# Softplus by ScalarE's table, the scan started three wide tiles earlier, and the context normalization moved into the first two tiles

## The chip, the cores and the metric

The kernel runs on one core of a Trainium2 chip. Its time is the device time of that core in microseconds (us); the median of three runs before the change is 1597.76 us (1597.14 to 1597.82). The core has five engines that run side by side and wait for one another through semaphores: TensorE (PE; its weight loads are PEld), VectorE (DVE), ScalarE (ACT), GpSimd (POOL) and SyncE (SP). Each takes its own instructions strictly in the order of the program. DMAs are started from the queues of SP, ACT and POOL.

## The reference, cut to what matters

One decoder layer on four sequences of 512 tokens, width 512: attention, then a selective state-space branch, then a gated feed-forward with routed low-rank adapters. The part that the change touches is the state-space branch:

```
x    = silu(conv(in_proj(ctx)))                    # 512 channels x 512 tokens
dt   = softplus(dt_proj(x_proj(x)[:16]) + dt_bias)
A    = -exp(A_log)                                 # 16 states for each channel
for each token:
    state = state * exp(dt * A) + (dt * u) * B
    y     = sum over the 16 states of state * C
y    = (y + D * x) * silu(layernorm(tokens after attention))
```

The first stage of each sequence is `layernorm(x)`, the input of attention.

## The kernel before, in words

A batch is one of the four sequences. All data are f32. Each batch b passes these stages:

1. Input projection, convolution, B, C and the step sizes dt (`conv_tap`, `convolve`, `conv_gate`, `split_first`, `softplus_parts`).
2. Projections of q, k and v with rotation (`project`, `rotate`), in 11 places f.
3. Attention: 32 steps, two heads in each (`attention`). In a step PE computes scores, DVE takes the maxima (L1117), ACT takes exponentials (L622), PE transposes (L830), ACT moves (L634), and PE weighs the values.
4. Feed-forward, of 11 wide tiles f = 0..10 of 128 columns ("wide tile"). For each tile PE forms `base` (L890, 16 matmul instructions), then two adapter slots (L902, 4 instructions each), and `down_adapters` (L910, 4). ACT takes a silu (L674) and DVE a product (L1253) after each of these three; such a pair is an evaluation, named (f, 0), (f, 1), (f, 2). Its place in the order is (0,0), (0,1), (1,0), (0,2), (1,1), (2,0), (1,2) and so on; `EVAL` holds it. PE's `base(f+2)` waits for the product of (f, 2), since both use the same PSUM banks.
5. Down products (L970), 11 places f, and a last one (L977), after which DVE adds the residual (L1266, `finish`).

Batch b+1's stages 1 and 2 and its scan run beside batch b's stages 4 and 5: stage 1 at the head of the feed-forward, the scan's pieces in DVE's and ACT's gaps from there on, stage 2's projections between the down products (one f of each), and the rest of the scan in batch b+1's attention. Batch 0 has nothing to hide behind: its scan runs beside its own projections and attention.

The scan of a batch goes over its 16 states n. For each n DVE does three pieces over 128 x 2048: mul (L1077, dt*u times B), run (L1082, the recurrence), out (L1087, times C). Then a DMA from POOL's queue adds the result to y (L484); the adds of a batch are serial, and the state has two buffers, so mul n waits until add n-2 has landed. ACT makes the decay factors of each n with four exponentials (L580), and loads B and C of each n by DMA (L570). Both wait in ACT's order for pieces of n-2. Ahead of the 48 scan pieces stand 12 "poly" pieces on DVE: softplus as max(v, 0) + log(1 + exp(-|v|)), where ACT gives |v|, its exponential and max(v, 0) (L546, L549, L551), and DVE evaluates a polynomial of degree 9 in Horner's form (L1051, nine times L1054), adds the two parts (L1059), and forms dt*u (L1063).

The order is fixed by tables written out by hand: `plan(counts)` deals the 60 pieces of a batch in order into slots, so many to each, and puts the loads and decays of n in a slot between the pieces that free and use their buffers, after an evaluation (f, 1) if one lies between. `PLAN_NEXT` (batches 1 to 3) has no piece before the fifth evaluation slot, from then on 2 pieces after (f, 1) and 1 after (f, 2), 22 pieces beside the down products, and the last 8 in attention. `PLAN_FIRST` (batch 0) has 13 pieces beside the projections, 10 of them in the first two places, and 47 in attention's first 31 steps. The normalization of batch b+1's attention input (`deviation`, L1014 to L1020, POOL's power L474, `scaled`, L1024) stands in `NORM_SLOTS`: one of four token tiles after (5, 2), (6, 2), (7, 2) and (8, 2) each.

## Time and profile before

| | |
|---|---|
| median of 3 runs | 1597.76 us |
| the profiled execution, its own time | 1596.27 us |
| its span in the profile | 1594.5 us |
| busy: PE, DVE, ACT, POOL | 1382.6, 1108.9, 689.2, 112.0 us |
| mean granted TensorE clock | 0.888 of full |

In order of time, batch 0's projections and attention fill about 0 to 270 us; then three periods of some 370 us follow, each with a feed-forward head (from 272 us), wide tiles (310 to 450), down products (450 to 527), attention of the next batch (536 to 620) and gating; the last feed-forward alone runs from 1390 to the end. A row of the timeline gives start, duration, engine, line, operation, output <- inputs, and how many instructions were merged; in brackets stands the idle time of the engine before it and what ended it. PE's clock stands at one of two levels, 2.4 GHz (1.00 in the rows) or 1.2 GHz (0.50).

### The profile page before, as it was taken

What the parts mean: (1) busy time and instruction counts of PE and PEld (TensorE: products, weight loads), DVE (VectorE), ACT (ScalarE), POOL (GpSimd) and SP (SyncE); (2) the same over time, 40 slices, a digit from 0 to 9 for tenths busy, and PEclk for the clock granted to TensorE, in tenths of its full rate; (3) what the DMA queues carried; (4) which work ended last, traced back from release to release, by engine and by line L of the source; (5) the groups of instructions that cost most, each with busy time, mean ns of one, the idle gap of its engine ahead of it and who ended that gap; (6) DMA issues with size and microseconds to landing.
All of it is one profiled execution on the core that took longest, in us unless ns stands there. A gap on an engine that the chain in (4) does not pass through costs nothing.

```text
span 1594.5 us, 16051 instructions
## 1 busy us (share of the span) xinstructions
PE 1382.6 (87%) x5768; PEld 675.0 (42%) x5768; DVE 1108.9 (70%) x1247; ACT 689.2 (43%) x1501; POOL 112.0 (7%) x116
## 2 busy tenths in 40 slices
PE   6756667999988799899989699899989698799999
PEld 2334334444443355434444255444434255454443
DVE  4899996557989775737999866637998967621120
ACT  6155653344543484343552376361562277321110
POOL 0000001000200000000210000100210000100000
PEclk8955558999999699999999778999999869789999
DMA  4166662114667631113766722002566751101112
GB/s 191 40 152 157 141 142 50 42 50 112 172 145 172 171 68 27 40 35 81 180 147 159 196 67 54 27 32 80 141 150 152 169 139 28 27 19 61 50 35 84
DMA packets 53277, 158.80 MB, mean 100 GB/s; under 512 B 5072, under 2 KB 10704, under 8 KB 44752
## 3 DMA queue, kind: packets, MB, share of 16 engines
q0 software_dynamic: 9216, 67.11, 20.4%
q1 hardware_dynamic: 25664, 54.23, 10.1%
q10 hardware_dynamic: 18320, 36.45, 8.6%
q8 instruction: 47, 0.77, 0.2%
q14 instruction: 30, 0.25, 0.0%
HBM read 86.20 MB, written 4.46 MB: 57 GB/s over the span
## 4 chain that ended last, share of the span: by engine, by line
issue 30%; PE 29%; DVE 26%; DMA 7%; ACT 5%; POOL 2%; ACTq 0%; DVEq 0%; POOLq 0%
DVE state L1082 10%; DMA y_sb<-state 7%; PE ps_a L890 5%; PE ps_a L970 4%; DVE state L1077 4%; PE ps_w L869 3%; DVE state L1087 3%; PE ps_a L816 3%; PE ps_a L902 2%; PE ps_b L830 2%; ACT r L622 2%; POOL rstd L474 2%; DVE neg_max L1117 2%; PE ps_b L910 2%; PE ps_w L778 2%
## 5 line engine op out<-in xcount | busy, mean ns | idle before, releaser
L890 PE MATMUL ps_a<-xt,w_sb 128*128 128x512 f32 x704 | 316.1, 603 | 0.0
L1082 DVE TENSOR_TENSOR_SCAN state<-decay,state 128x2048 f32<-128x2048 f32 x64 | 282.8, 4419 | 7.5 <-ACT decay L580 3.4
L1253 DVE TENSOR_TENSOR r<-r,ps_a 128x512 f32<-128x512 f32 x132 | 88.6, 683 | 206.4 <-ACT r L674 206.4
L816 PE MATMUL ps_a<-r 32*128 32x512 f32 (+3 forms) x512 | 140.6, 634 | 84.0 <-ACT r L622 57.5
L890 PEld LDWEIGHTS ps_a<-xt,w_sb 128*128 128x128 f32 x704 | 135.6, 194 | 171.1 <-issue 171.1
L674 ACT ACTIVATE r<-ps_a 128x512 f32<-128x512 f32 x132 | 78.4, 597 | 297.8 <-PE ps_a L902 158.7
L580 ACT ACTIVATE decay<-dt_sb,decay_rate 128x511 f32<-128x511 f32 x256 | 163.0, 712 | 63.2 <-DVE state L1087 31.2
L622 ACT ACTIVATE r<-ps_a,neg_max 128x128 f32<-128x128 f32 (+3 forms) x256 | 133.8, 534 | 118.7 <-DVE neg_max L1117 118.3
L902 PE MATMUL ps_a<-r,wb_sb 128*128 128x512 f32 x352 | 166.7, 596 | 11.1 <-DVE r L1253 8.9
L970 PE MATMUL ps_a<-wd_sb,r 128*128 128x512 f32 x352 | 161.8, 611 | 0.8 <-DMA wd_sb<-in_w_down 0.8
L1077 DVE TENSOR_TENSOR state<-du_sb,bc_sb 128x2048 f32<-128x2048 f32 x64 | 146.3, 2287 | 5.2 <-DMA y_sb<-state 5.0
L1087 DVE TENSOR_TENSOR state<-state,bc_sb 128x2048 f32<-128x2048 f32 x64 | 146.0, 2281 | 0.7
L830 PE MATMUL ps_b<-cst,r 128*128 128x128 f32 x640 | 120.4, 331 | 25.6 <-ACT xt L634 17.2
L1117 DVE TENSOR_REDUCE neg_max<-ps_a 128x2 f32<-128x256 f32 (+3 forms) x128 | 104.0, 814 | 19.9 <-PE ps_a L819 19.0
L484 POOL DMA_DIRECT2D y_sb<-state x64 | 56.1, 877 | 738.1 <-DVE state L1087 653.4
L902 PEld LDWEIGHTS ps_a<-r,wb_sb 128*128 128x128 f32 x352 | 64.9, 190 | 101.9 <-issue 95.1
L970 PEld LDWEIGHTS ps_a<-wd_sb,r 128*128 128x128 f32 x352 | 69.1, 198 | 88.7 <-issue 84.0
L830 PEld LDWEIGHTS ps_b<-cst,r 128*128 128x128 f32 x640 | 89.1, 172 | 34.5 <-issue 28.7
L816 PEld LDWEIGHTS ps_a<-r 32*128 32x128 f32 x512 | 50.2, 239 | 120.7 <-ACT r L622 79.7
L474 POOL TENSOR_TENSOR rstd<-var_eps,cst 128x1 f32<-128x1 f32 x48 | 56.0, 1167 | 543.7 <-DVE var_eps L1020 534.3
L910 PE MATMUL ps_b<-r,ad_sb 128*128 128x512 f32 x176 | 85.8, 611 | 1.9 <-DVE r L1253 1.7
L1054 DVE SCALAR_TENSOR_TENSOR du_sb<-du_sb,state 128x2048 f32<-128x2048 f32 x36 | 82.4, 2288 | 0.6
(123 smaller groups left out, 1448.4 us busy)
## 6 DMA issues: line engine op xcount, KB each, us to landing
y_sb<-state POOLq DMA_DIRECT2D x64, 1024.0 KB, 9.7
bc_sb<-bc_rows ACTq DMA_DIRECT2D x64, 512.0 KB, 5.1
w_sb<-in_w_tiles SPq DMA_DIRECT2D x44, 512.0 KB, 4.0
wd_sb<-in_w_down SPq DMA_DIRECT2D x44, 256.0 KB, 3.6
wb_sb<-in_w_adapt SPq DMA_DIRECT2D x44, 128.0 KB, 2.1
xa<-in_x SPq DMA_DIRECT2D x4, 1024.0 KB, 5.2
out_x<-xb SPq DMA_DIRECT2D x16, 256.0 KB, 7.0
xn_att<-in_ctx_t SPq DMA_DIRECT2D x4, 512.0 KB, 6.1
```

The lines of the kernel that those rows point to most:

```text
L580: nc.scalar.activation(decay[:, n % 2, j, 1:L], dt_sb[:, j, 1:L], ACT.Exp, scale=decay_rate[:, j, n:n + 1]).then_inc(decay_ready, 1)
L622: nc.scalar.activation(probs[:, (2 * s + k) % 4, 0:(i + 1) * P], score_place(s, k), ACT.Exp, bias=neg_max[:, s % 2, k:k + 1], accum_out=ro ...
L816: nc.tensor.matmul(score_place(s, k), q_t[rows, m, i * P:(i + 1) * P], k_t[rows, 0:width], start=True, stop=False, tile_position=(rows.sta ...
L830: mm = nc.tensor.transpose(ps_b[:, k, kt * P:(kt + 1) * P], probs[:, (2 * s + k) % 4, kt * P:(kt + 1) * P], ident)
L890: mm = nc.tensor.matmul(ps_a[:, 2 * (f % 2) + half, :], w_sb[:, slot, at + k * P:at + (k + 1) * P], xt[:, k, :], start=(k == 0), stop=Fals ...
L902: mm = nc.tensor.matmul(ps_a[:, 2 * (f % 2) + half, :], wb_sb[:, f % 2, at:at + P], low[:, 2 * half + k - 1, :], start=False, stop=(k == 2 ...
L910: mm = nc.tensor.matmul(ps_b[:, k - 1, :], ad_sb[:, f, :], hk[:, (2 * f + k - 1) % 4, :], start=(f == 0), stop=(f == FT - 1), skip_group_c ...
L970: mm = nc.tensor.matmul(ps_a[:, i, :], hb[:, f, i * P:(i + 1) * P], wd_sb[:, f % 2, :], start=(f == 0), stop=False, skip_group_check=True)
L1077: tt(state[:, n % 2, :, :], du_sb[:], row, ALU.mult).then_inc(scan_chain, 1)
L1082: nc.vector.tensor_tensor_scan(flat, decay[:, n % 2, :, :].rearrange("p j l -> p (j l)"), flat, 0.0, ALU.mult, ALU.add).then_inc(scan_chai ...
L1087: tt(state[:, n % 2, :, :], state[:, n % 2, :, :], row, ALU.mult).then_inc(scan_chain, 1)
L1117: nc.vector.tensor_reduce(neg_max[:, s % 2, :], both, AX.X, ALU.max, negate=True)\
```

## The change

- Softplus is one ScalarE activation for each channel tile, straight from PSUM into `dt_sb`. The 12 poly pieces become one, "du", which forms dt*u; 49 pieces are left of 60. The scratch uses of `exp_v` and `relu_v` go.
- For batches 1 to 3 the first piece comes after (1, 1): two pieces there, none after (1, 2), and from tile 2 on 2 after (f, 1) and 1 after (f, 2) as before. 29 pieces stand there (30 before), 13 beside the down products (22 before), 7 in attention (8 before).
- For batch 0: one piece in each of the 11 places beside the projections, 38 in attention (47 before).
- The normalization of the next attention input is done in two pairs of token tiles, after (0, 1) and after (0, 2).

```diff
-    pieces = [("poly", k) for k in range(NPOLY + 2)]
+    pieces = [("du", 0)]
...
-        slots[between(at["poly", NPOLY - 4] if n < 2 else at["out", n - 2], at["mul", n])]["bc"].append(n)
-        slots[between(at["poly", NPOLY + 1] if n < 2 else at["run", n - 2], at["run", n])]["decay"].append(n)
+        slots[at["du", 0] if n < 2 else between(at["out", n - 2], at["mul", n])]["bc"].append(n)
+        slots[between(at["du", 0] if n < 2 else at["run", n - 2], at["run", n])]["decay"].append(n)
...
-NORM_SLOTS = [EVAL_AT[FT - 2 - NT + i, 2] for i in range(NT)]
+NORM_AT = {EVAL_AT[0, 1]: (0, 1), EVAL_AT[0, 2]: (2, 3)}
...
-IN_EVALS = [(0, 2, 1)[k] if e >= POLY_AT and f <= LAST_TILE else 0 for e, (f, k) in enumerate(EVAL)]
-IN_DOWN = 22 
+IN_EVALS = [0 if f == 0 else ((0, 2, 0) if f == 1 else (0, 2, 1))[k] for f, k in EVAL]
+IN_DOWN = 13
...
-            def softplus_parts(b, tiles):
+            def softplus(b, tiles):
                 for j in tiles:
                     bank = filled(act, ("dt", j), b)
...
+                    nc.scalar.activation(dt_sb[:, j, :], ps_w[:, bank, :], ACT.Softplus,
+                                         bias=vec[:, V_DTB + j:V_DTB + j + 1]).then_inc(work_free[bank], 1)
...
+                if kind == "du":
+
+                    for j in (JT - 2, JT - 1):
+                        bank, count = use(("dt", j), b)
+                        dve.wait_ge(work_free[bank], count + 1)
+                    dve.wait_ge(u_ready, b * JT + JT)
+                    tt(du_sb[:], dt_sb[:], u_sb, ALU.mult).then_inc(du_ready, 1)
+
+                    nc.vector.memset(decay[:, :, :, 0:1], 0.0).then_inc(dt_ready, 1)
...
-                    if e in NORM_SLOTS:
+                    for i in NORM_AT.get(e, ()):
                         dve.wait_ge(loaded["x"], 16 * t + 32)
-                        deviation("att", t + 1, xa, NORM_SLOTS.index(e))
+                        deviation("att", t + 1, xa, i)
+                    for i in NORM_AT.get(e, ()):
+                        scaled("att", t + 1, xa, xn_att, i)
                     for piece in PLAN_NEXT[e]["dve"]:
                         scan_piece(t + 1, piece)
-                    if e in NORM_SLOTS:
-                        scaled("att", t + 1, xa, xn_att, NORM_SLOTS.index(e))
```

How this moves the instructions, at three places. First, ACT between the evaluations of tiles 0 and 1 of a feed-forward; L674 is a silu before the change, L549 the exponential of softplus. Before:

```order
L674 ACTIVATE r<-ps_a 128x512 x2
L546 ACTIVATE state<-ps_w,vec 128x512
L549 ACT_TABLE_LOAD
L549 ACTIVATE state<-state 128x512
L551 ACTIVATE decay<-ps_w,vec 128x512
L546 ACTIVATE state<-ps_w,vec 128x512
L549 ACTIVATE state<-state 128x512
L551 ACTIVATE decay<-ps_w,vec 128x512
L674 ACT_TABLE_LOAD
L674 ACTIVATE r<-ps_a 128x512
```

After it; L642 is the silu, L522 the softplus, L548 a decay, L538 the loads of B and C:

```order
L642 ACTIVATE r<-ps_a 128x512
L522 ACT_TABLE_LOAD
L522 ACTIVATE dt_sb<-ps_w,vec 128x512 x2
L642 ACT_TABLE_LOAD
L642 ACTIVATE r<-ps_a 128x512
L538 DMA bc_sb<-bc_rows 128x2x512 x2
L642 ACTIVATE r<-ps_a 128x512
L548 ACT_TABLE_LOAD
L548 ACTIVATE decay<-dt_sb,decay_rate 128x511 x4
L642 ACT_TABLE_LOAD
L642 ACTIVATE r<-ps_a 128x512 x2
```

Three activations for each pair member became one, and the first decay stands after the silu of (2, 0), ahead of that of (1, 2); before the change the first decays stood behind the polynomial, four tiles later.

Second, DVE in the same tiles. Before (L1253 is the product of an evaluation, L1051 and L1054 are the polynomial):

```order
L1253 TENSOR_TENSOR r<-r,ps_a 128x512 x4
L1051 TENSOR_SCALAR du_sb<-state 128x2048
L1054 SCALAR_TENSOR_TENSOR du_sb<-du_sb,state 128x2048
L1253 TENSOR_TENSOR r<-r,ps_a 128x512 x2
L1054 SCALAR_TENSOR_TENSOR du_sb<-du_sb,state 128x2048
L1253 TENSOR_TENSOR r<-r,ps_a 128x512
L1054 SCALAR_TENSOR_TENSOR du_sb<-du_sb,state 128x2048 x2
```

After (L1211 is the product, L992 ends a normalization pair, L1021 is du, L1035, L1040 and L1045 are mul, run and out):

```order
L992 TENSOR_SCALAR xn_att<-xa,mv,rstd 128x512 x2
L1211 TENSOR_TENSOR r<-r,ps_a 128x512
L1021 TENSOR_TENSOR du_sb<-dt_sb,state 128x2048
L1023 MEMSET decay 128x8
L1035 TENSOR_TENSOR state<-du_sb,bc_sb 128x2048
L1211 TENSOR_TENSOR r<-r,ps_a 128x512 x3
L1040 SCALAR_TENSOR_TENSOR state<-decay,state 128x2048
L1045 TENSOR_TENSOR state<-state,bc_sb 128x2048
L1211 TENSOR_TENSOR r<-r,ps_a 128x512 x2
L1035 TENSOR_TENSOR state<-du_sb,bc_sb 128x2048
L1211 TENSOR_TENSOR r<-r,ps_a 128x512
```

The scan's first pieces stand where the polynomial's stood, and each tile from the third on has run and out after one product, mul after the next two.

Third, DVE at the end of the down products, from the last rotation (L1103 before, L1061 after) to the residual sum of `finish` (L1266, L1224). Before:

```order
L1103 TENSOR_TENSOR r<-r 128x512
L1082 SCALAR_TENSOR_TENSOR state<-decay,state 128x2048
L1087 TENSOR_TENSOR state<-state,bc_sb 128x2048
L1077 TENSOR_TENSOR state<-du_sb,bc_sb 128x2048
L1082 SCALAR_TENSOR_TENSOR state<-decay,state 128x2048
L1108 COPY v_sb<-ps_b 128x256
L1087 TENSOR_TENSOR state<-state,bc_sb 128x2048
L1077 TENSOR_TENSOR state<-du_sb,bc_sb 128x2048
L1082 SCALAR_TENSOR_TENSOR state<-decay,state 128x2048
L1087 TENSOR_TENSOR state<-state,bc_sb 128x2048
L1077 TENSOR_TENSOR state<-du_sb,bc_sb 128x2048
L1266 TENSOR_TENSOR xb<-ps_a,xb 128x512 x4
```

After:

```order
L1061 TENSOR_TENSOR r<-r 128x512
L1045 TENSOR_TENSOR state<-state,bc_sb 128x2048
L1035 TENSOR_TENSOR state<-du_sb,bc_sb 128x2048
L1040 SCALAR_TENSOR_TENSOR state<-decay,state 128x2048
L1066 COPY v_sb<-ps_b 128x256
L1045 TENSOR_TENSOR state<-state,bc_sb 128x2048
L1035 TENSOR_TENSOR state<-du_sb,bc_sb 128x2048
L1040 SCALAR_TENSOR_TENSOR state<-decay,state 128x2048
L1224 TENSOR_TENSOR xb<-ps_a,xb 128x512 x4
```

Ten pieces between the last rotation and `finish` became seven, and fewer stand ahead of that rotation. PE's order is the same in both kernels; on POOL the powers of a batch's normalization now all stand ahead of its adds. SP's order is unchanged.

## Rows read from the trace of the kernel before

**Rows 1.** Part 1 of the page: engine, busy us, share, instructions.
```profile
PE 1382.6 (87%) x5768; PEld 675.0 (42%) x5768; DVE 1108.9 (70%) x1247; ACT 689.2 (43%) x1501; POOL 112.0 (7%) x116
```

**Rows 2.** Stretches: from:to, us, busy of PE, PEld, DVE, ACT, POOL; clock, DMA, GB/s.
```profile
78.00:120.00 42.00, 24.72 (x132) 12.95 (x132) 41.79 (x29) 25.39 (x68) 2.77 (x3) 0.57 0.59 145
...
450.50:514.50 64.00, 56.21 (x131) 24.41 (x129) 57.61 (x35) 17.97 (x28) 5.22 (x6) 0.97 0.67 160
...
536.00:558.60 22.60, 21.56 (x114) 11.02 (x114) 13.94 (x20) 14.97 (x48) 0.00 (x0) 0.50 0.58 178
558.60:575.00 16.40, 15.85 (x206) 10.07 (x202) 11.03 (x22) 13.25 (x49) 0.86 (x1) 1.00 0.42 98
```

**Rows 3.** Groups by line: instructions, busy us and mean ns, idle before.
```profile
L1082 DVE TENSOR_TENSOR_SCAN state<-decay,state 128x2048 f32<-128x2048 f32 x64 | 282.8, 4419 | 7.5 <-ACT decay L580 3.4
...
L1087 DVE TENSOR_TENSOR state<-state,bc_sb 128x2048 f32<-128x2048 f32 x64 | 146.0, 2281 | 0.7
...
L1054 DVE SCALAR_TENSOR_TENSOR du_sb<-du_sb,state 128x2048 f32<-128x2048 f32 x36 | 82.4, 2288 | 0.6
...
L674 ACT ACT_TABLE_LOAD x28 | 35.9, 1283 | 0.5
...
L546 ACT ACTIVATE state<-ps_w,vec 128x512 f32<-128x512 f32 x16 | 10.9, 680 | 1.1 <-PE ps_w L752 1.1
```

**Rows 4.** Timeline of batch 0: DVE's first rows, and POOL's second and last add.
```profile
36.37 1.23 DVE L1051 TENSOR_SCALAR du_sb<-state 128x2048 f32<-128x2048 f32 x1 [9.96 <-ACT scrap_a L555]
...
80.10 0.42 DVE L1117 TENSOR_REDUCE neg_max<-ps_a 128x2 f32<-128x256 f32 x1
...
98.19 0.88 POOL L484 DMA_DIRECT2D y_sb<-state  x1 [9.42 <-DMA y_sb<-state]
...
247.53 0.88 POOL L484 DMA_DIRECT2D y_sb<-state  x1 [9.35 <-DVE state L1087]
```

**Rows 5.** PE's timeline: `base` of wide tiles 4, 5, 8 and 9.
```profile
352.89 7.03 PE L890 MATMUL ps_a<-xt,w_sb 128*128 128x512 f32 x16
...
364.91 7.03 PE L890 MATMUL ps_a<-xt,w_sb 128*128 128x512 f32 x16
...
401.38 7.03 PE L890 MATMUL ps_a<-xt,w_sb 128*128 128x512 f32 x16
...
414.18 7.03 PE L890 MATMUL ps_a<-xt,w_sb 128*128 128x512 f32 x16
```

**Rows 6.** DVE's timeline: mul of three tiles; then POOL's powers, ns min/median/max.
```profile
417.61 2.29 DVE L1077 TENSOR_TENSOR state<-du_sb,bc_sb 128x2048 f32<-128x2048 f32 x1
...
430.40 2.29 DVE L1077 TENSOR_TENSOR state<-du_sb,bc_sb 128x2048 f32<-128x2048 f32 x1
...
441.19 2.28 DVE L1077 TENSOR_TENSOR state<-du_sb,bc_sb 128x2048 f32<-128x2048 f32 x1
...
L474 POOL TENSOR_TENSOR rstd<-var_eps,cst x12: 550/780/2531, 388.4 to 650.5; 128x1 f32<-128x1 f32 x12
```

**Rows 7.** Timeline: PE at the dt products in tile 0; ACT's decay in tile 7.
```profile
323.58 1.13 PE L752 MATMUL ps_w<-xdt_sb,wdt_sb 128*128 128x512 f32 x2 [0.72 <-ACT decay L551]
...
326.36 1.88 PE L902 MATMUL ps_a<-r,wb_sb 128*128 128x512 f32 x4
...
392.25 2.56 ACT L580 ACTIVATE decay<-dt_sb,decay_rate 128x511 f32<-128x511 f32 x4
```

**Rows 8.** PE's timeline at the end of the down products.
```profile
514.55 1.12 PE L799 MATMUL ps_b<-cst,r 128*128 128x128 f32 x4 [7.03 <-ACT r L608]
...
523.36 3.60 PE L977 MATMUL ps_a<-bd_sb,r 128*128 128x512 f32 x8
536.06 0.80 PE L816 MATMUL ps_a<-r 32*128 32x128 f32 x4 [9.10 <-DVE xb L1266]
```

**Rows 9.** PE's timeline late in that attention, around a wait.
```profile
608.82 1.24 PE L816 MATMUL ps_a<-r 32*128 32x512 f32 x4 [2.71 <-ACT r L622]
...
611.60 2.08 PE L816 MATMUL ps_a<-r 32*128 32x512 f32 x4
```

More of the change, by code:

```diff
@@ L43 @@
 VD = KV_HEADS * HD
-def log1p_coefficients(degree):
-    import numpy as np
-    nodes = 0.5 + 0.5 * np.cos(np.pi * (np.arange(64) + 0.5) / 64)
-    fit = np.polynomial.Chebyshev.fit(nodes, np.log1p(nodes) / nodes, degree, domain=[0, 1])
-    return [float(c) for c in fit.convert(kind=np.polynomial.Polynomial).coef]
-POLY = log1p_coefficients(9)
-NPOLY = len(POLY)
 EVAL = [(0, 0)]
@@ L72 @@
 SLOTS = ATT + STEPS
-NORM_SLOTS = [EVAL_AT[FT - 2 - NT + i, 2] for i in range(NT)]
+NORM_AT = {EVAL_AT[0, 1]: (0, 1), EVAL_AT[0, 2]: (2, 3)}
 DT_SLOTS = (2, 3)
-POLY_AT = 4
-LAST_TILE = FT - 1
 PV_AT = 5
@@ L256, in decoder_layer @@
         xdt_sb = sb("xdt_sb", [P, L])
-        u_sb, exp_v, relu_v, conv_sb = state[:, 0, :, :], state[:, 1, :, :], decay[:, 0, :, :], decay[:, 1, :, :]
-        xin_sb = relu_v
+        u_sb, xin_sb, conv_sb = state[:, 0, :, :], decay[:, 0, :, :], decay[:, 1, :, :]
         scrap = sb("scrap", [1, 1])
@@ L323, in decoder_layer @@
         bc_stored = sem("bc_stored")
-        softplus_chain = sem("softplus_chain")
-        softplus_in = sem("softplus_in")
         y_init = sem("y_init")
-        poly_chain = sem("poly_chain")
+        du_ready = sem("du_ready")
         dt_ready = sem("dt_ready")
@@ L500, in _ @@
                 for e in range(EVALS):
-                    inverse_deviation("att", t + 1, [i for i in range(NT) if NORM_SLOTS[i] == e])
+                    inverse_deviation("att", t + 1, NORM_AT.get(e, ()))
                     add_states(t + 1, PLAN_NEXT[e])
@@ L691, in _ @@
             split_first(0)
-            softplus_parts(0, range(JT))
+            softplus(0, range(JT))
             for f in range(FT):
@@ L712, in _ @@
                     scan_inputs(t + 1, PLAN_NEXT[e])
-                    softplus_parts(t + 1, [j for _, j in dt_uses(e)])
+                    softplus(t + 1, [j for _, j in dt_uses(e)])
                 for f in range(FT):
@@ L1070, in scan_piece @@
                     if n == 0:
-                        dve.wait_ge(poly_chain, (b + 1) * (NPOLY + 2))
+                        dve.wait_ge(du_ready, b + 1)
                         dve.wait_ge(y_init, b * JT + JT)
```

35 lines of the change are left out of this document (2 added, 33 removed).

## The prediction

> **What bounds the kernel now.** I read the page's first part, then a table of stretches by stage, then PE's and DVE's timelines where a stretch looked full. DVE is busy for only 70% of the span [rows 1], but that is a mean over unlike stages. In batch 0's attention it is busy 41.79 of 42.00 us while PE stands at about half its clock and is busy for 24.72 [rows 2]: DVE sets the pace, and stays full until its last scan piece ends at about 247 us, where the last add starts [rows 4]. In the wide tiles PE sets the pace, one tile in 364.91 - 352.89 = 12.02 us, except where the normalization stands: 414.18 - 401.38 = 12.80 us [rows 5]. Beside the down products DVE is busy 57.61 of 64 us, and PE twice waits for what is queued behind DVE's pieces: 7.03 us at the turning of v, 9.10 us before the first scores [rows 2, 8]. The attention that follows starts at half clock: 22.6 us for its first eight steps with PE busy 21.56, against 16.4 us for the next eight at full clock [rows 2]. The last feed-forward runs alone and is not touched.
>
> **The change part by part.**
>
> *Work removed.* Ten polynomial pieces and one addition leave each batch. The nine L1054 alone are 9 x 2.288 = 20.6 us a batch, 82.4 us in all [rows 3]. What this is worth depends on the stage.
>
> *Softplus.* No row shows this function. One activation from PSUM with a bias column takes 0.68 us (L546), the sequence of three now in place about three times that [rows 3]; it could be no cheaper than nothing. I take 0.68 us, since the shape and operands are those of L546; the upper end would cost 16 x 1.3 us more on ACT, on the path only in the first dozen, near 5 us in all. Each change of function set shows as one load of 1.283 us [rows 3]; 91 stand in the new order against 66.
>
> *Batch 0.* Now DVE starts the polynomial at 36.37 us, having waited 9.96 us, and takes the first maxima at 80.10 [rows 4]. After the change eight activations of some 0.55 us, overlaps taken off, leave ACT's row, so softplus ends about 4 us earlier, near 32.3, du (2.3 us) near 34.6, and then the projections pace DVE: B and C of n = 0 land near 42 us (their issue follows the four moves of the transposed tokens), the first two decays sit on ACT between the first and second q move, and out 1 falls near 73. mul 3 is the last piece before the maxima, and waits until add 1 has landed, one add later: adds follow each other in (247.53 - 98.19)/14 = 10.7 us [rows 4], so near 84, and it ends near 86.2. The first maxima come 6.1 us later than now. From there 38 pieces remain instead of 47: three runs, outs and muls fewer. A run is 4.42 us, an out 2.28 and a mul 2.29 [rows 3, 6], less an overlap of about 0.1 us each: 3 x 8.8 = 26.3 us. Balance -20.2 us; I take 1 us off for waits that show when each step holds less DVE work: **-19 us**. Bounds: -12 (DVE waits for PE at half clock) and -24 (the start loses nothing).
>
> *Wide tiles of batches 1 to 3.* Three terms.
> Softplus at tile 0: PE waits for free banks at the dt products (323.58) and starts the slot of (1, 1) at 326.36 [rows 7]; without waits the four groups end at 324.42, so PE would gain 1.9 us.
> It gives this back at once. The first decay stands between the silus of (2, 0) and (1, 2). It costs two loads and 2.56 us [rows 3, 7] = 5.1 us, so the product of (1, 2) is ready about 2.2 us after `base(3)` wants it. Balance at tile 3: -0.25 us. Bounds -2 and +3.
> The normalization leaves tiles 5 to 8: its three full tiles cost 0.78 us each over 12.02 [rows 5], the first, by the same difference, 0.42, together 2.75 us. In tile 0 a pair stands between two products with a `base` of 6.9 us of PE between them, where DVE has nothing else; each half of it costs what the tiles show, 2.0 us [rows 6], so a pair takes 4 us and is hidden.
> Tiles 2 to 4 trade polynomial for scan. A DVE cycle with three scan pieces and three products, no normalization, takes 441.19 - 430.40 = 10.8 us, with it 430.40 - 417.61 = 12.8 [rows 6]. 10.8 is below PE's 12.02. Inside a tile the product of (f+1, 0) comes after run and out, 8.9 us after the slot of (f, 1) ends; PE wants it at 10.3 (`base` 6.87, slot 1.72, adapters 1.72). Cover 1.4 us; nothing is lost. Together **-3.0 us** a batch.
>
> A power on POOL takes 0.55 us at best and 2.53 us in the tiles where DVE's out runs beside it [rows 6]. By the Trainium skill ("SBUF — State Buffer", "Who interferes with whom") a VectorE instruction with two SBUF inputs holds off a GpSimd one that reads SBUF; this trace agrees, and by that rule the moved powers, beside statistics of one input, take the short time.
>
> *Down products.* From PE's own work, matmul pairs at 0.86 us: after the place of the last raw projection but one nothing holds PE, so L799 comes at 507.4 (now 514.55), L977 at 515.1 (now 523.36, 1 us of it low clock) and ends at 518.5, on the clock of batch 1 [rows 8]. DVE has 13 pieces, 39 us, in a stage where it had 22. I followed it place by place: after the rotation of place 6 (500.6) come out 11 (502.9), mul 12, run 12 (509.6), the copy of v (510.0), out 12 (512.3). mul 13 waits for add 11, 502.9 + 10.7 = 513.6, and ends at 515.9; run 13 ends at 520.3. ACT loads B and C of 13 behind out 11 at 502.9, before the move of v is due at 503.9: it just fits. So the residual sums start at 520.3 and the first scores, which need two, at 521.7 against 536.06 [rows 8]: **-14.4 us**. Bounds: -9 (ACT's queue still holds v back) and -16.5 (PE's end decides). One weight load of the down products is late by 0.8 us today and stays so; the one of place 10 has only 4.3 us from its release and may be 3 us late, which DVE's end covers.
>
> *Attention of batches 1 to 3.* One run leaves the first eight steps, seven pieces remain. At half clock PE is bound there (21.56 of 22.6 us), so the run is worth about **-1 us**. If the clock stays full the eight steps take what the next eight do, -6.1 us. For a fall: a wait of 2.71 us late in the same attention, followed by scores on 32 rows, was enough; the same matmuls that had taken 1.24 us took 2.08 from 611.60 on [rows 9]. My timeline leaves PE idle for up to 3.2 us at this place, followed by the same sparse matmuls. I take a fall.
>
> **Sum.** -19 + 3 x (-3.0 - 14.4 - 1.0) = -19 - 55.2 = -74.2 us. The profiled execution took 1596.27 us (span 1594.5, 1.8 us around it), which gives 1522.1; the median is 1.5 us above the profiled execution, so 1523.5.
>
> **The rivals.**
> *The clock stays full after the shortened gap.* For it: the gap shrinks from 9.1 us to 3 or less, and to nothing if a late weight load fills it with work. Against it: rows 9. Worth 3 x 5.1 = 15.3 us more: 1508.
> *Only part of the down gain comes.* The queue of adds or ACT's loads, which wait in order for out n-2, hold the move of v or mul 13 by some 5 us; batch 0 meets the adds' pace and gains 12. For it: the margins above are 1 to 2 us, and DMA engines are 67% busy there [rows 2]. Sum: -12 - 3 x 13 = -51: 1546.
> *ACT becomes the bound by its loads.* 25 more loads are 32 us of ACT; at 1.28 us each they lie in silu gaps. If each switch held ACT twice as long, the stall of `base(3)` would grow by 2.6 us and the two softplus pairs by as much: 3 x 5.2 = 15.6 us, 1539. The rows speak against it: a decay group such as the one at 392.25 follows its load with no idle time before it [rows 7].
> By the Trainium skill ("ScalarE: Activation LUTs", "What ACT_TABLE_LOAD costs") a switch costs about 2.66 us, a drain on top of the load; the load itself agrees with the row, the drain is not seen here.
> *Slower.* The scan triple now stands in nine tiles more or less densely from tile 2 on, so 27 tiles depend on mul n finding add n-2 landed. Out ends 8.2 us into its tile, mul comes 22.0 us after that tile's start: an add may take 13.8 us. Now it takes 10.7 from one to the next [rows 4]. Were it 17.5 us, 27 tiles would lose 3.7 us each, 100 us, and the time would be 1624; below 13.8 nothing is lost. Break-even stands near 16.5 us.
>
> **How the numbers follow.** Forecast 0.56, clock full 0.26, partial gain 0.11, ACT bound 0.03, slower 0.02, and 0.02 for a gain eaten by something unseen. The range runs from the clock rival with a little more in batch 0 (1501) to the partial gain (1545) and leaves out less than 0.2; the forecast's own range is 1514 to 1534. About 0.2% is what a measurement of this kernel tells from none: faster 0.96, same 0.01, slower 0.03.
>
> **What would show it.** Batch 0: first maxima near 86, last scan piece near 227. Tiles: `base` every 12.02 us from tile 3 on, one PE wait of about 2 us before `base(3)`. Down: no wait of PE at the turning of v, first scores 14 us earlier, clock 0.50 in the steps after. The prediction fails if PE shows waits in every tile (then DVE or ACT is late), or if the last scan piece of batch 0 does not move by about 20 us.

## The result and the profile after

The changed kernel takes 1528.68 us (median of four runs, 1524.95 to 1531.99) against 1597.79 us of the kernel before in the same session: a ratio of 0.956, with a 95% interval from 0.952 to 0.959. The forecast was 1523.5 us, 5 us less. The profiled execution took 1529.66 us, its span 1527.9 us: 66.6 us less than before, where the sum said 74.2.

Part 1 of the page after, and the row below it on which engine stands on the chain that ended last. They answer to [rows 1].

```profile
PE 1373.7 (90%) x5768; PEld 678.7 (44%) x5768; DVE 1018.1 (67%) x1203; ACT 704.4 (46%) x1490; POOL 89.7 (6%) x116
...
PE 68%; DVE 19%; ACT 6%; DMA 3%; issue 3%; ACTq 0%; POOL 0%; DVEq 0%
```

DVE lost 91 us of work and ACT gained 15; PE's share of the chain is 68%. To see where the time went, I took the starts of four groups in PE's timeline (first scores, L784; output projection, L837; `base(0)`, L858; first down product, L938) in both traces, and subtracted stage by stage. The three figures of a stage are batches 1 to 3, or feed-forwards 0 to 2:

| stage | before, us | after, us | difference | forecast |
|---|---|---|---|---|
| batch 0 up to `base(0)` | 288.0 | 266.4 | -21.6 | -19 |
| wide tiles | 162.5, 164.0, 163.7 | 160.8, 160.9, 160.8 | -7.6 | -9.0 |
| down products up to the first scores | 85.6, 84.6, 85.4 | 70.1, 70.3, 70.8 | -44.5 | -43.2 |
| attention up to the output projection | 80.6, 81.4, 81.4 | 86.3, 82.5, 79.6 | +5.1 | -3.0 |
| gating and head | 41.2, 41.0, 42.9 | 41.0, 41.0, 42.2 | -0.9 | 0 |
| last feed-forward alone | 192.2 | 195.1 | +2.9 | 0 |

Three of four terms came within 3 us of the forecast. The fourth has the wrong sign. Attention's 32 steps, in groups of eight (start of the first scores to start of the next group's; the last group ends at the output projection), the three figures again batches 1 to 3:

| steps | before, us | after, us | difference |
|---|---|---|---|
| 0 to 7 | 22.5, 22.5, 22.5 | 20.2, 16.2, 14.7 | -16.4 |
| 8 to 15 | 16.4, 17.1, 17.3 | 19.0, 19.2, 19.7 | +7.2 |
| 16 to 23 | 19.2, 19.7, 19.8 | 18.6, 18.8, 17.3 | -4.1 |
| 24 to 31 | 22.4, 22.1, 21.8 | 28.4, 28.3, 27.9 | +18.3 |

Stretches of after, for the first eight steps of attention, the next three groups of eight (batch 1), and the first and last group of batch 3; then the kernel before's last group of batch 1. The columns are those of [rows 2].

```profile
497.34:517.56 20.22, 18.82 (x112) 9.82 (x113) 10.61 (x19) 13.78 (x47) 0.86 (x1) 0.62 0.76 222
517.56:536.60 19.04, 16.49 (x205) 10.67 (x201) 14.39 (x22) 13.27 (x49) 0.00 (x0) 0.95 0.01 2
536.60:555.22 18.62, 18.62 (x201) 12.39 (x201) 10.76 (x21) 15.16 (x53) 0.88 (x1) 0.82 0.29 59
555.22:583.65 28.43, 26.61 (x204) 15.35 (x200) 16.44 (x25) 17.29 (x57) 0.87 (x1) 0.59 0.05 10
...
1210.90:1225.60 14.70, 12.02 (x112) 6.55 (x112) 10.35 (x19) 11.68 (x43) 0.87 (x1) 1.00 0.71 220
...
1262.61:1290.50 27.89, 23.30 (x205) 14.03 (x201) 16.45 (x25) 16.99 (x57) 0.86 (x1) 0.70 0.05 11
```

```profile
594.18:616.62 22.44, 19.18 (x201) 11.77 (x201) 16.65 (x24) 16.46 (x57) 0.87 (x1) 0.85 0.03 7
```

The last eight steps take 28 us in all three batches where they took 22, with the same DVE work (16.44 against 16.65 us) and, in batch 1, 7.4 us more of PE: PE is not given more work, it runs at half clock for most of the group (0.59 on average). What stands in front of it is in the merged timeline of after, PE, DVE and ACT at the turn to that group:

```profile
553.64 2.27 DVE L1035 TENSOR_TENSOR state<-du_sb,bc_sb 128x2048 f32<-128x2048 f32 x1
...
555.83 1.22 DVE L1075 TENSOR_REDUCE neg_max<-ps_a 128x2 f32<-128x1024 f32 x1
...
557.08 0.69 ACT L590 ACTIVATE r<-ps_a,neg_max 128x512 f32<-128x512 f32 x1 [1.19 <-DVE neg_max L1075]
...
558.58 0.49 PE L784 MATMUL ps_a<-r 32*128 32x128 f32 x4 [1.78 <-ACT r L590]
...
562.35 1.22 PE L784 MATMUL ps_a<-r 32*128 32x256 f32 x4
```

A mul stands ahead of the maxima of the widest scores (1024 columns), so its exponential and with it the next narrow scores are late; PE idles 1.78 us, and the scores on 256 columns, four of which take 0.70 us at 2.4 GHz, take 1.22: 1.2 GHz from about there. In batch 3 the clock is low for a shorter part (0.70), and the group takes as long, since PE waits once more, behind the run at step 26:

```profile
1278.06 1.65 PE L784 MATMUL ps_a<-r 32*128 32x384 f32 x4 [2.78 <-ACT r L590]
```

Taking one piece out of attention had moved the others: `spread_over(8, 31)` put the last seven at steps 7, 11, 15, 19, 23, 27, 30, all but the last behind the second maxima of a pair; `spread_over(7, 31)` puts them at 4, 8, 13, 17, 22, 26, 30.

### The profile page after: what moved, and what is told of

It is laid out like the page before. It is cut to its first block, busy times and chain, and to the rows that moved or that the text cites. A ratio compares the mean times of both kernels' runs of the same rounds, so it can differ in the third digit from the quotient of the medians.

```text
span 1527.9 us, 15994 instructions
## 1 busy us (share of the span) xinstructions
PE 1373.7 (90%) x5768; PEld 678.7 (44%) x5768; DVE 1018.1 (67%) x1203; ACT 704.4 (46%) x1490; POOL 89.7 (6%) x116
## 3 DMA queue, kind: packets, MB, share of 16 engines
q0 software_dynamic: 9216, 67.11, 22.1%
q1 hardware_dynamic: 25664, 54.23, 10.6%
## 4 chain that ended last, share of the span: by engine, by line
PE 68%; DVE 19%; ACT 6%; DMA 3%; issue 3%; ACTq 0%; POOL 0%; DVEq 0%
PE ps_a L858 20%; PE ps_a L870 9%; DVE state L1040 7%; PE ps_a L938 7%; PE ps_b L878 5%; PE ps_a L784 4%; PE ps_w L746 4%; PE ps_w L837 4%; PE ps_b L798 3%; DMA y_sb<-state 3%; DVE state L1035 2%; DVE neg_max L1075 2%; PE ps_w L904 2%; PE ps_w L813 2%; ACT r L590 2%
## 5 line engine op out<-in xcount | busy, mean ns | idle before, releaser
L858 PE MATMUL ps_a<-xt,w_sb 128*128 128x512 f32 x704 | 318.7, 607 | 6.4 <-DVE r L1211 6.4
L1040 DVE TENSOR_TENSOR_SCAN state<-decay,state 128x2048 f32<-128x2048 f32 x64 | 282.6, 4416 | 1.3
L858 PEld LDWEIGHTS ps_a<-xt,w_sb 128*128 128x128 f32 x704 | 136.5, 195 | 180.1 <-issue 180.1
L1211 DVE TENSOR_TENSOR r<-r,ps_a 128x512 f32<-128x512 f32 x132 | 90.2, 685 | 188.5 <-ACT r L642 188.5
L642 ACT ACTIVATE r<-ps_a 128x512 f32<-128x512 f32 x132 | 78.4, 596 | 268.2 <-PE ps_a L858 122.5
L548 ACT ACTIVATE decay<-dt_sb,decay_rate 128x511 f32<-128x511 f32 x256 | 163.3, 710 | 71.0 <-DVE state L1040 70.6
L784 PE MATMUL ps_a<-r 32*128 32x512 f32 (+3 forms) x512 | 138.7, 626 | 54.5 <-ACT r L590 50.6
L938 PE MATMUL ps_a<-wd_sb,r 128*128 128x512 f32 x352 | 156.6, 594 | 8.1 <-DMA wd_sb<-in_w_down 8.1
L1035 DVE TENSOR_TENSOR state<-du_sb,bc_sb 128x2048 f32<-128x2048 f32 x64 | 146.0, 2282 | 10.2 <-DMA bc_sb<-bc_rows 5.2
L1045 DVE TENSOR_TENSOR state<-state,bc_sb 128x2048 f32<-128x2048 f32 x64 | 146.2, 2285 | 1.4
L798 PE MATMUL ps_b<-cst,r 128*128 128x128 f32 x640 | 123.7, 339 | 15.6 <-ACT r L602 9.2
L938 PEld LDWEIGHTS ps_a<-wd_sb,r 128*128 128x128 f32 x352 | 67.0, 192 | 93.3 <-issue 80.1
L798 PEld LDWEIGHTS ps_b<-cst,r 128*128 128x128 f32 x640 | 92.8, 178 | 22.1 <-issue 20.0
L784 PEld LDWEIGHTS ps_a<-r 32*128 32x128 f32 x512 | 49.2, 234 | 89.8 <-ACT r L590 66.0
L602 ACT ACTIVATE xt<-ps_b 128x256 f32<-128x256 f32 (+1 forms) x128 | 58.3, 500 | 26.3 <-PE ps_b L798 25.6
L1088 DVE TENSOR_TENSOR r<-ps_w,r 128x128 f32<-128x128 f32 x64 | 18.3, 286 | 68.1 <-ACT r L609 68.1
```

The source lines that it names most:

```text
L548: nc.scalar.activation(decay[:, n % 2, j, 1:L], dt_sb[:, j, 1:L], ACT.Exp, scale=decay_rate[:, j, n:n + 1]).then_inc(decay_ready, 1)
L784: nc.tensor.matmul(score_place(s, k), q_t[rows, m, i * P:(i + 1) * P], k_t[rows, 0:width], start=True, stop=False, tile_position=(rows.sta ...
L798: mm = nc.tensor.transpose(ps_b[:, k, kt * P:(kt + 1) * P], probs[:, (2 * s + k) % 4, kt * P:(kt + 1) * P], ident)
L858: mm = nc.tensor.matmul(ps_a[:, 2 * (f % 2) + half, :], w_sb[:, slot, at + k * P:at + (k + 1) * P], xt[:, k, :], start=(k == 0), stop=Fals ...
L938: mm = nc.tensor.matmul(ps_a[:, i, :], hb[:, f, i * P:(i + 1) * P], wd_sb[:, f % 2, :], start=(f == 0), stop=False, skip_group_check=True)
L1035: tt(state[:, n % 2, :, :], du_sb[:], row, ALU.mult).then_inc(scan_chain, 1)
```

## Experiments

All kernels are variants of the changed kernel. Medians are of 4 to 10 runs, ratios are to the kernel before on the same chip. The intervals reach 0.2 to 0.4% to either side: runs of one variant differ by 4 to 16 us, those of the kernel before on one chip by 23, and the longer ones mostly have the lower granted clock (after: 1524.95 us at 0.907, 1531.99 at 0.899). The median of the kernel before is 1596.6 to 1599.9 us on the four chips, so medians of two variants from different chips can lie 3 us apart for that alone.

**The attention pieces at the steps of before.**

```diff
-                 spread_over(PIECES - sum(IN_EVALS) - IN_DOWN, STEPS - LAST_STEPS) + [0] * LAST_STEPS)
+                 [int(s in (7, 11, 15, 19, 23, 27, 30)) for s in range(STEPS)])
```

> The changed kernel, with the same seven scan pieces of batches 1 to 3 in attention, now behind the maxima of steps 7, 11, 15, 19, 23, 27 and 30, where the kernel before had the same seven; the changed kernel has them at 4, 8, 13, 17, 22, 26, 30. Nothing else differs. Theory P (positions): in the changed kernel a mul behind the first wide step (22) and a run at 13 hold up the maxima of the next wide step, PE waits 1.8 and 2.6 us for exponentials at the narrow scores that follow, the granted clock falls there, and the last eight steps take 28 us. Then here the waits before the first scores of the third and fourth group of eight go below 0.6 us, the second group takes 16.5 us (now 19.0 to 19.7) and the last 22.4 (now 28), and the three attentions together take 20 to 25 us less: about 1506 us. Rival C (the clock falls for what came before attention): the waits go, but the low stretches stay, and the time is 1525 or more. Rival N: seven pieces cost what they cost, no attention gets shorter by over 1 us.

Measured 1511.91 us, ratio 0.947 (0.944 to 0.949): 17 us less than the changed kernel. Its four groups of eight in batch 1, and the first group of batch 3:

```profile
502.35:522.35 20.00, 18.81 (x113) 9.81 (x112) 9.52 (x18) 12.94 (x45) 0.00 (x0) 0.62 0.39 134
522.35:539.45 17.10, 16.60 (x204) 10.70 (x200) 11.06 (x21) 13.17 (x49) 0.86 (x1) 0.95 0.43 94
539.45:559.15 19.70, 17.82 (x202) 11.08 (x200) 14.48 (x22) 14.84 (x53) 0.88 (x1) 0.91 0.27 55
559.15:581.20 22.05, 18.81 (x208) 11.42 (x200) 16.67 (x24) 16.49 (x57) 0.87 (x1) 0.87 0.03 6
1202.38:1215.70 13.32, 11.92 (x114) 6.60 (x114) 8.43 (x18) 11.77 (x43) 0.00 (x0) 1.00 0.51 180
```

The last group is back at 22.05 us, the second at 17.1; the third gives back 1 us. Theory P (the positions) holds, in the size a little less than expected (17 us of 20 to 25; the three attentions are 18 us shorter together). The 8 us by which the attention term was off are this, and more.

**The normalization back in tiles 5 to 8.**

```diff
-NORM_AT = {EVAL_AT[0, 1]: (0, 1), EVAL_AT[0, 2]: (2, 3)}
+NORM_AT = {EVAL_AT[FT - 2 - NT + i, 2]: (i,) for i in range(NT)}
```

(and `scaled` again behind the scan pieces of the slot.)

> The changed kernel with the normalization of the next attention input back behind the evaluations (5,2), (6,2), (7,2) and (8,2), a token tile in each. The prediction's term: the period of base in those tiles goes from 12.02 to 12.8 us in three of them and 12.4 in one, 2.75 us a batch, about 8 us in all: 1537. Rival: since VectorE now also waits less elsewhere, or since the tiles' end is set by what follows them, nothing comes of it (1529), or, with the scan already running in these tiles as before, more than 4 us a batch (1541 or more).

Measured 1541.99 us, ratio 0.965 (0.961 to 0.969): 13 us more. Two stretches from one `base` to the next:

```profile
370.53:382.68 12.15, 12.15 (x30) 5.24 (x28) 11.59 (x12) 6.91 (x9) 2.86 (x3) 1.00 0.71 199
382.68:395.41 12.73, 12.26 (x30) 5.24 (x29) 12.17 (x12) 6.91 (x9) 3.43 (x3) 1.00 0.73 181
```

POOL's powers in these tiles (ns: least, median, most):

```profile
L451 POOL TENSOR_TENSOR rstd<-var_eps,cst x3: 2547/2547/2549, 382.5 to 407.9; 128x1 f32<-128x1 f32 x3
```

PE's timeline at the last down product of feed-forward 2:

```profile
1213.52 6.75 PE L938 MATMUL ps_a<-wd_sb,r 128*128 128x512 f32 x8 [2.73 <-DMA wd_sb<-in_w_down]
```

The period is 12.73 us as it was 12.80 [rows 5], and the wide tiles lose 2.0 us a batch, 5.9 in all: the term was 2.75 a batch. The three periods from `base(7)` to `base(10)` lose 1.6 of these 2.0. The profiled execution is 17.6 us longer than that of the changed kernel (it is the slowest of its four), and most of that is not in the tiles. The down products took 4.3 us more, where the clock fell, as the last row shows (eight matmuls in 6.75 us behind a late weight load; 3.7 us behind the same wait in the changed kernel). Attention took 4.3 us more: its first eight steps 20.2 us in all three batches, where the changed kernel's trace has 20.2, 16.2 and 14.7, and its last eight 26.4 instead of 28. Batch 0, which the edit does not touch, took 2.8 us more. So the time is that of the rival that expected over 4 us a batch, but the trace gives the place 2.0; whether the edit has a part in the rest is open. The powers stand beside a mul here, beside an out in the kernel before; in the changed kernel the powers beside the statistics took 0.547 to 0.782 us. By the Trainium skill ("SBUF — State Buffer", "Who interferes with whom") a VectorE instruction with two SBUF inputs contends with a GpSimd one that reads SBUF; both traces agree.

**The scan started late, 22 pieces beside the down products.**

```diff
-IN_EVALS = [0 if f == 0 else ((0, 2, 0) if f == 1 else (0, 2, 1))[k] for f, k in EVAL]
-IN_DOWN = 13
+IN_EVALS = [0 if f < 4 else ((0, 2, 0) if f == 4 else (0, 2, 1))[k] for f, k in EVAL]
+IN_DOWN = 22
```

> The changed kernel with the scan starting behind (4,1) instead of (1,1): 20 pieces in the wide tiles instead of 29, 22 beside the down products instead of 13, the same seven in attention at the same steps. Theory: the down products' 15 us a batch hang on the number of pieces there, since v's move and the residual sums stand behind them; the stage from the first down product to the first scores goes from 70.3 back to about 85 us, PE waits 7 us at the turning of v and 8 to 9 us before the first scores: 3 x 14.7 = 44 us more, 1573. Base(3) starts 2.1 us earlier, since no decay stands before it: 1567. Rival: part of the 15 us came from the queue of adds and from ScalarE's order, not from the count; then the stage stays under 78 us, 1550 or less.

Measured 1590.87 us, ratio 0.996 (0.994 to 0.998): 62 us more, so that nearly all of the change's gain is gone. The stage of the down products and the eight steps of attention behind it:

```profile
428.17:514.60 86.43, 67.61 (x160) 29.51 (x158) 80.29 (x44) 24.11 (x40) 6.08 (x7) 0.93 0.74 167
514.60:536.10 21.50, 21.24 (x114) 10.97 (x114) 10.53 (x19) 14.12 (x47) 0.86 (x1) 0.50 0.72 212
```

The stage takes 86.4 us as before the change: the number of pieces there decides, worth 16.3 us a batch, 49 in all. Against the expected 1567 the kernel is 24 us slower. The wide tiles, from which 6 us were to come, are 2.4 us longer together: the wait before `base(3)` is gone, but it moved with the scan's start to `base(6)`, which comes 14.31 us after `base(5)`, and the period after it takes 13.79 us. The attentions are 11 us longer together. Their first eight steps start at half clock and take 21.5 us; most variants with 13 pieces have 20.0 to 21.3, so the changed kernel's trace, with its 16.2 and 14.7, was lucky there, and only some 1 us a batch goes to the low start.

**Batch 0 alone put back.**

```diff
-PLAN_FIRST = plan([0] * DOWN + [1] * FT + spread_over(PIECES - FT, STEPS - LAST_STEPS) + [0] * LAST_STEPS)
+PLAN_FIRST = plan([0] * DOWN + [2] + [0] * (FT - 1) + spread_over(PIECES - 2, STEPS - LAST_STEPS) + [0] * LAST_STEPS)
```

> The changed kernel, batch 0 alone altered: 2 pieces beside its projections and 47 in its attention, as the attention of the kernel before had, instead of 11 and 38. Theory: VectorE bounds this attention, nine pieces cost 3 x 8.8 = 26.3 us, and the first maxima come some 6 to 10 us earlier: 17 to 20 us more, about 1547. Rival: with the shorter softplus ahead, attention is bound by TensorE at half clock, and nine pieces more cost under 10 us: 1538 or less.

Measured 1547.47 us, ratio 0.969 (0.966 to 0.971): 19 us more. In the trace batch 0 accounts for 10.6 of the 15.8 us between the two spans (`base(0)` at 277.0 instead of 266.4); the rest is spread over the later stages, nowhere over 4 us. First maxima of this kernel, and of the changed one with the mul ahead of them:

```profile
69.23 0.42 DVE L1075 TENSOR_REDUCE neg_max<-ps_a 128x2 f32<-128x256 f32 x1 [0.89 <-PE ps_a L787]
```

```profile
84.97 2.29 DVE L1035 TENSOR_TENSOR state<-du_sb,bc_sb 128x2048 f32<-128x2048 f32 x1 [1.46 <-DMA y_sb<-state]
87.18 0.42 DVE L1075 TENSOR_REDUCE neg_max<-ps_a 128x2 f32<-128x256 f32 x1
```

With two pieces instead of 11 beside the projections the first maxima come 18 us earlier, but the scores before them only 8.5; attention from its first scores is 14.8 us longer, the gating behind it 4.3. The 19 us of the medians agree with the expected 17 to 20, but its terms did not come: 18 us less before the first maxima for 6 to 10, and 10.6 us in batch 0, where the expectation put all of it. The other 5 us between the spans are in stages that the edit does not touch. The arrangement is worth half of batch 0's gain, the shorter softplus at its head the other half (80.1 to 69.2 us for the first maxima).

**The softplus alone, in the arrangement of before.** The diffs of the last three kernels together, with 19 pieces in the wide tiles and 8 in attention.

> The softplus activation alone, in the arrangement of the kernel before: the normalization in tiles 5 to 8, 19 pieces in the wide tiles (du behind (4,1), the scan from tile 5), 22 beside the down products, 8 in attention at the steps of the kernel before; batch 0 with 2 pieces beside the projections and 47 in attention. Theory (the ten polynomial pieces were hidden, the gain is in where the scan's pieces moved): base(0) of batch 0 starts 11 us earlier than in the kernel before, as in the kernel with batch 0 alone put back; the rest of a batch is within 2 us of before: 1581 to 1587. Rival (the removed 82 us of VectorE are themselves the gain): under 1560. Rival (nothing was on the path): 1595 or more.

Measured 1591.26 us, ratio 0.995 (0.992 to 0.998). The 8.6 us are less than the 11 to 17 expected: batch 0 gives its 9.9 us, and two of the three stages of wide tiles are longer than before, by 3.6 and 1.2 us, with the same wait before `base(6)` as with the late scan (2.12 us). In batches 1 to 3 the ten polynomial pieces were hidden, and their removal pays through the places that it opens; in batch 0, where nothing hides them, it pays at once.

**The decay of n = 0 behind the silu of (1, 2)**, on top of the old attention steps.

```diff
+        s = between(at["du", 0] if n < 2 else at["run", n - 2], at["run", n])
+        slots[s + (n == 0 and s < EVALS)]["decay"].append(n)
```

> The kernel with the seven attention pieces at the steps of before (1511.9 us), and the decay of n = 0 in the feed-forwards behind the silu of (1,2) instead of ahead of it. Theory: the prediction's cause of the stall of base(3) is right; PE's wait of 2.13 us before it goes, base(3) follows base(2) by 12.0 to 12.4 instead of 14.3 us, and nothing takes its place: 3 x 2.1 = 6 us less, 1505.5. Rival: run 0 then waits for its decay and holds the products behind it, and the wait shows up at base(4) instead: 1512.

Measured 1512.26 us, ratio 0.946 (0.942 to 0.949): no gain over 1511.91. PE's `base(2)` and `base(3)` in the changed kernel and `base(2)` to `base(4)` in this one, then its late weight load in batch 2:

```profile
304.53 7.03 PE L858 MATMUL ps_a<-xt,w_sb 128*128 128x512 f32 x16
318.84 7.10 PE L858 MATMUL ps_a<-xt,w_sb 128*128 128x512 f32 x16 [2.13 <-DVE r L1211]
```

```profile
305.48 7.03 PE L859 MATMUL ps_a<-xt,w_sb 128*128 128x512 f32 x16
317.50 7.03 PE L859 MATMUL ps_a<-xt,w_sb 128*128 128x512 f32 x16
...
330.56 7.03 PE L859 MATMUL ps_a<-xt,w_sb 128*128 128x512 f32 x16
...
837.94 6.71 PE L939 MATMUL ps_a<-wd_sb,r 128*128 128x512 f32 x8 [2.82 <-DMA wd_sb<-in_w_down]
```

The stall is gone (12.02 us from `base(2)` to `base(3)`), and 1.04 us of it stands at `base(4)`: 1.3 us a batch is gained. It is lost again: behind the late load of place 10 the clock fell, and with its eight matmuls at up to 6.71 us the stage took 73.2 us in two batches of three, 2.6 and 3.0 more than before the move. That the move made the clock fall is not shown: the same wait, 2.4 to 2.9 us, stands in every trace with two buffers and 13 pieces, and the eight matmuls behind it took 3.70 us in some batches and 5.2 to 6.75 in others.

**A run at step 23 instead of 27.** Only the list of steps differs: 7, 11, 15, 19, 21, 23, 27.

> The changed kernel with its seven attention pieces at steps 7, 11, 15, 19, 21, 23, 27: against the version with the steps of before (1511.9 us) the mul of n = 15 moves from 23 to 21, its run from 27 to 23, its out from 30 to 27. Theory: a run costs nothing behind the last wide step of a group, as the one at 15, and a wait of 2.7 us behind the run at 27; with that wait gone the granted clock stays at 1.00 in the last group of eight, which takes 18 to 19 us instead of 22; the third group takes up to 1 us more: 3 x 2.5 = 7 us less, 1504. Rival: the low clock at the end of attention comes without the wait too, or the run at 23 costs at the narrow steps behind it what it cost at 27: 1510 to 1514.

Measured 1510.80 us, ratio 0.945 (0.941 to 0.949). The last group of eight, against 22.05 us above:

```profile
554.48:574.20 19.72, 17.88 (x201) 11.09 (x201) 14.51 (x23) 14.86 (x53) 0.87 (x1) 0.91 0.27 54
```

The mechanism is seen: the wait of 2.7 us is gone, the group takes 19.7 us, and the gating behind it 39.4 instead of 41.0. The third group gives back 0.5. From that some 3 us a batch should follow, and the medians show 1 in all. Their runs overlap (1503.7 to 1514.4 and 1509.4 to 1515.8), and they come from two chips: the time is not settled by them. The traces say why little may show: without the first eight steps, attention and gating are 9 us shorter over the three batches, but the older trace had one batch whose first eight steps took 13.3 us instead of 20.

**Batch 0's doubled pieces at other steps**: `[1 + int(s in (7, 11, 15, 19, 23, 27, 30)) for s in range(STEPS - LAST_STEPS)]`.

> The kernel with the seven attention pieces at the steps of before (1511.9 us), and in batch 0's attention the seven steps that hold two pieces are 7, 11, 15, 19, 23, 27, 30 instead of 4, 8, 13, 17, 22, 26, 30. Theory: here too it matters before which maxima a pair of pieces stands; with the pairs off the steps ahead of wide scores batch 0's attention, 146.5 us, takes 3 to 8 us less: about 1507. Rival: VectorE is the bound there whatever the step, since its pieces and maxima fill the stage: within 1 us, 1512.

Measured 1510.42 us, ratio 0.945 (0.941 to 0.949). Batch 0's attention takes 146.7 us as it did with 146.5: the rival holds. In the changed kernel DVE is busy for 143.88 of its 146.66 us; where DVE is full, this change of their order was worth nothing.

**Three buffers for the down products' weights**, on the steps of the kernel with the run at 23 (`wd_sb` and its semaphores by f % 3, a load waits for f - 3).

> The version with the attention pieces at 7, 11, 15, 19, 21, 23, 27 (1510.8 us), with three buffers for the weights of the down products instead of two, so that the load for place 10 is released a place earlier. Theory (the prediction's: the load of place 10, late by 2.4 to 2.9 us, is covered by VectorE's end): PE's wait goes, the first scores come at most 0.5 us earlier, since run 13 ends when it did; the time stays within 2 us of 1510.8, except where the late load let the clock fall, as it did in two of three batches of the kernel with the decay moved, where the eight matmuls behind it took 6.7 instead of 3.7 us. Rival (the late load is on the path): 3 x 2.4 = 7 us less, 1503.6, the stage of the down products 68 us instead of 70.4.

Measured 1511.91 us, ratio 0.944 (0.942 to 0.947). Place 10 and what follows it in the changed kernel and in this one:

```profile
489.53 3.70 PE L938 MATMUL ps_a<-wd_sb,r 128*128 128x512 f32 x8 [2.43 <-DMA wd_sb<-in_w_down]
493.07 3.60 PE L945 MATMUL ps_a<-bd_sb,r 128*128 128x512 f32 x8
497.34 0.49 PE L784 MATMUL ps_a<-r 32*128 32x128 f32 x4 [0.67 <-DVE xb L1224]
```

```profile
835.71 7.03 PE L938 MATMUL ps_a<-wd_sb,r 128*128 128x512 f32 x16
842.58 3.60 PE L945 MATMUL ps_a<-bd_sb,r 128*128 128x512 f32 x8
849.31 0.49 PE L784 MATMUL ps_a<-r 32*128 32x128 f32 x4 [3.14 <-DVE xb L1224]
```

The wait moved, unshortened, from the load to DVE's end (2.43 + 0.67 = 3.10 us before, 3.14 now). The load was covered, as the prediction said. (The first rows are of batch 1, the others of batch 2; there the changed kernel's waits were 2.74 and 0.58 us.)

**One piece less beside the down products**: `IN_DOWN = 12`, attention pieces at 3, 7, 11, 15, 19, 21, 23, 27.

> The kernel with three buffers for the down products' weights, with 12 pieces beside the down products instead of 13, and 8 in attention, at 3, 7, 11, 15, 19, 21, 23, 27. Theory: with the load in time PE's end decides the stage as soon as VectorE holds one run (4.4 us) less there: first scores 2.4 to 3 us earlier, the stage of the down products about 67.5 us; the run at step 3 of attention costs 1 to 1.5 us if the clock is low there and less than 0.5 at full clock, where nothing waits for it: 3 x 1.5 = 4 us less than with 13. Rival: VectorE's pieces cost the same wherever they stand, or the run at step 3 takes back what the stage gives: no difference to 13 beyond 1.5 us.

Measured 1500.02 us, ratio 0.938 (0.935 to 0.940), runs from 1499.3 to 1503.8:

```profile
772.30:839.36 67.06, 66.70 (x160) 29.50 (x158) 49.22 (x34) 14.79 (x24) 3.47 (x4) 1.00 0.53 125
839.36:860.36 21.00, 19.13 (x113) 9.81 (x113) 13.98 (x20) 14.64 (x48) 0.00 (x0) 0.60 0.64 191
```

PE is busy for 66.70 of 67.06 us: the stage is at PE's own time. The first eight steps take 21.0 us with the run at step 3, against 21.3 with 13 pieces. In batch 3 the clock was still full when that run held up the maxima, and PE waited for it:

```profile
1195.75 2.08 PE L784 MATMUL ps_a<-r 32*128 32x512 f32 x4 [3.03 <-ACT r L590]
```

The group took 21.0 us there too. So at low clock the run costs under 1 us (with 13 pieces such groups took 20.0 to 21.3), and at full clock it did not cost less, as expected, but brought a wait of 3 us. The gain is 12 us where 4 were expected; the stages of the down products account for 3.1 us a batch, 9.3 in all. Twelve pieces with two buffers were not run. By the changed kernel's rows the late load would hold PE back by 2.4 to 2.9 us of these 3.1, an estimate.

**The decay moved as well**, with 13 pieces and with 12.

> The kernel with three buffers for the down products' weights and 13 pieces there, and with the decay of n = 0 behind the silu of (1,2). Theory: the decay's move gained 1.1 to 2.1 us in each wide stage when it was tried and lost 2.5 in the down stage where the late load let the clock fall; with the load in time only the gain is left: 3 x 1.5 = 4.5 us less than the same kernel without the move. Rival: the down stage gets longer by the gain again, since its end is tied to something that the move doesn't change, such as the chain of adds: no difference beyond 1 us.

> The fastest kernel so far (three buffers for the down products' weights, 12 pieces beside them, 8 in attention, 1500.0 us) with the decay of n = 0 behind the silu of (1,2). Theory: each wide stage is 1.1 to 2 us shorter, as it was in the two kernels with this move (156.3 to 159.7 us against 160.5 to 161.5), nothing else changes: 1495 to 1497. Rival: what the wide stage gives is taken back by the granted clock, which stood lower (0.904 against 0.906 to 0.917) in the kernels with this move: 1499 to 1505, with a wider spread of its runs than the 4.5 us of the kernel without it.

With 13 pieces 1510.02 us, ratio 0.942 (0.938 to 0.945); with 12, 1493.11 us, ratio 0.933 (0.930 to 0.936), the fastest kernel of the study, 2.3% under the changed one. Each theory has something: the stages of wide tiles take 157.7 to 160.3 us, and in both profiles one group of eight steps fell to 0.64 and 0.67 of the clock and took 26 to 27 instead of 20 us. Its own gain is not settled: with 13 pieces it is 1.9 us by the medians, with 12 it is 6.9, from another chip, and in both cases the intervals with and without the move overlap. With 12 pieces the runs spread from 1490.0 to 1502.6.

## Why the prediction was right, and where it was not

- *Batch 0, -19.* -21.6. Softplus ended at 33.1 (32.3 said), the first maxima came at 87.2 (86.2), and the last scan piece ended at 227.1 (227). mul 3 waited 1.46 us for the add, as said. From the first maxima on nine pieces less were worth 26.3 us by the forecast; with all nine back the same stretch is 27 us longer (69.2 to the last add at 236.5, against 87.2 to 227.5).
- *Wide tiles, -3.0 a batch.* -2.5. `base` came every 12.02 us from tile 4 on (12.09 from tile 3 to 4), and the wait before `base(3)` was 2.13 us for 2.2. The normalization alone measured 2.0 for 2.75.
- *Down products, -14.4 a batch.* -14.8. Its reason, the count of DVE pieces ahead of v's move and the residual sums, is shown from both sides: 22 pieces 86.4 us, 13 pieces 70.3, 12 pieces 67.1. The forecast's bound of -16.5 (PE's end decides) lies close to what 12 pieces give with three buffers, 67.1 against 85.2: -18.
- *Attention, -1.0 a batch.* This is the step that failed, by its sign: +1.7 on average. The average hides two errors. The first eight steps gave 5.5 us a batch where 1.0 was forecast, and the other 24, put at nothing, cost 7.2. "One run leaves the first eight steps, seven pieces remain" took the seven as standing still. They moved, and only the order says where: a mul ahead of the widest maxima and a run at step 13 let PE wait 1.8 and 2.6 us, and the clock fell during or just behind the waits. The steps put back gave 17 us. For the first eight steps the forecast took a fall of the clock from their start (0.50) against the rival of a full one. Neither is what came: all three batches started at full clock, which then fell after 4.8 us for 17, after 4.7 us for 7, or not at all, and the steps took 20.2, 16.2 and 14.7 us in one execution. The mechanism, that a gap of up to 3.2 us brings half clock at once, did not hold; that the steps came out short made up, by luck, for much of the 21 us that the moved pieces cost.
- *Last feed-forward, 0.* +2.9 us, all in its first two wide tiles, with the same instructions and a clock of 0.97 for 0.99 over the wide tiles. Why the clock stood lower is open.
- *ACT bound by its loads.* Not so. 91 loads stand in the trace as counted, each 1.283 us, with softplus 0.01 us behind its load (7 times); in 62 of the 91 the next activation follows within 0.02 us, and in the others it waits for PE, DVE or a DMA. The Trainium skill's 2.66 us a switch ("ScalarE: Activation LUTs", "What ACT_TABLE_LOAD costs") does not show here.

Groups by line of the changed kernel, as in [rows 3], then the start of softplus in a feed-forward:

```profile
L642 ACT ACT_TABLE_LOAD x40 | 51.3, 1283 | 0.7
L548 ACT ACT_TABLE_LOAD x34 | 43.6, 1283 | 0.6
...
L522 ACT ACTIVATE dt_sb<-ps_w,vec 128x512 f32<-128x512 f32 x16 | 10.2, 684 | 2.7 <-PE ps_w L720 2.6
L522 ACT ACT_TABLE_LOAD x7 | 9.0, 1283 | 0.1
```

```profile
298.48 1.28 ACT L522 ACT_TABLE_LOAD   x1
299.77 1.26 ACT L522 ACTIVATE dt_sb<-ps_w,vec 128x512 f32<-128x512 f32 x2
```

Softplus takes 0.684 us for each tile; 0.68 was taken.

- *Slower by the adds.* Not seen: the waits of mul for an add are 4.8 us over the whole span, 1.46 of them at mul 3 of batch 0.

## What to carry to other kernels

Work removed from an engine with idle time pays little by itself: the softplus alone was worth 0.5%, all of it in batch 0, where nothing hid it; the new arrangement of the other pieces was worth 4%. When a spread of pieces changes its count, print where each lands, and look at what stands behind it: a mul of 2.3 us ahead of the widest reduction cost 6 us of attention, where a whole run taken out was to save 1. Where two things are late at one point, as the weight load and DVE's end here, removing one can show nothing: the load alone gave none of the 3 us a batch that came once DVE's end went too.
